# First expert stage of a two-layer transformer: rows and places of a pair of tiles by one transfer each, and three other loads and stores moved to later tiles

## The reference

```
xn = layernorm(x)
x  = x + linear_attention(xn) + experts_top2(xn)              # layer 0
xn = layernorm(x)
x  = x + block_softmax_attention(xn) + experts_capacity(xn)   # layer 1
```

```
logits = xn @ router_w.T ;  top_vals, top_idx = top_k(logits, 2) ;  top_w = softmax(top_vals)
h = square(relu(xn @ w1[e]))          # 256 -> 512, for the chosen expert e
y = h @ w2[e]                         # 512 -> 256
out[token] = sum over its two experts of top_w * y
```

## Time and profile before

| what | value |
|---|---|
| median of three runs | 743.87 us (742.98 to 746.7) |
| the profiled execution: span from first to last instruction | 743.1 us (the profile gives no other time of it) |
| TensorE (PE) busy | 688.5 us, 93% of the span |
| VectorE (DVE) / ScalarE (ACT) / GpSimd (POOL) busy | 545.0 / 446.2 / 443.7 us |
| TensorE lines of the expert stage: L987 / L951 / L962 / L934 | 111.9 / 86.7 us for the two large ones; L962 and L934 are smaller |
| row loads (L572) and id loads (L576) | 71 each, 128 KB and 0.5 KB |

### The profile page before, as it was taken

The page is one execution under the profiler, slowest core; times in us unless marked ns, Lnnn a source line. Parts: engine busy times, 40 slices in busy tenths (PEclk is TensorE's granted clock), DMA queues, the critical chain, the costliest instruction groups (busy, mean ns, idle before and its releaser), DMA issues.

```text
span 743.1 us, 19839 instructions
## 1 busy us (share of the span) xinstructions
PE 688.5 (93%) x6400; PEld 619.2 (83%) x6400; DVE 545.0 (73%) x1311; ACT 446.2 (60%) x940; POOL 443.7 (60%) x524
## 2 busy tenths in 40 slices
PE   5999998899999899999998999799898899999993
PEld 4898877788999899999977999677677678888883
DVE  5999777766887677878658886699986686666632
ACT  6565476666776677745526888466676664444420
POOL 3577789698997897996422223034354635555363
PEclk9999999999999999999999999899999999999998
DMA  9689752365443434533169985145568755666252
GB/s 255 169 261 290 233 164 65 93 175 133 118 124 113 122 101 135 144 87 113 38 202 302 304 282 171 34 106 127 116 112 205 218 197 136 150 147 163 33 58 28
DMA packets 147015, 111.91 MB, mean 151 GB/s; under 512 B 59361, under 2 KB 137188, under 8 KB 146920
## 3 DMA queue, kind: packets, MB, share of 16 engines
q1 hardware_dynamic: 133720, 84.84, 41.4%
q0 software_dynamic: 12624, 25.35, 13.6%
q10 hardware_dynamic: 576, 0.53, 0.3%
HBM read 66.58 MB, written 40.80 MB: 145 GB/s over the span
## 4 chain that ended last, share of the span: by engine, by line
PE 64%; DVE 8%; issue 5%; ACT 3%; DMA 3%; POOL 2%; SPq 1%; ACTq 1%; POOLq 0%; DVEq 0%
PE banks L987 12%; PE bank L1243 11%; PE bank L951 9%; PE banks L1254 5%; PE bank L1043 5%; PE banks L878 4%; PE bank L962 4%; PE banks L1060 3%; PE bank L934 2%; PE bank L1133 2%; PE bank L1122 1%; PE bank L1150 1%; DVE rw L2031 1%; PE banks L865 1%; PE banks L1219 1%
## 5 line engine op out<-in xcount | busy, mean ns | idle before, releaser
L987 PE MATMUL banks<-r_split,rt_split 128*128 x852 | 111.9, 285 | 4.3 <-ACT rw L1447 1.6
L987 PEld LDWEIGHTS banks<-r_split,rt_split 128*128 128x128 f32 x852 | 105.2, 190 | 6.0 <-issue 5.9
L2385 POOL DMA_INDIRECT ults_by_choice_and_token<-rw,y_id x71 | 80.7, 1137 | 39.8 <-ACT rw L1447 29.1
L1243 PE MATMUL bank<-r_split 128*128 128x512 f32 x384 | 89.6, 391 | 1.3 <-issue 1.1
L951 PE MATMUL bank<-wq_high_or_w_low_split,rt_split 128*128 128x256 f32 x560 | 86.7, 286 | 0.6 <-DVE rt_split L1870 0.6
L2333 POOL DMA_INDIRECT rows_by_expert<-rw,slots x64 | 66.2, 1034 | 32.6 <-issue 16.2
L1243 PEld LDWEIGHTS bank<-r_split 128*128 128x128 f32 x384 | 71.4, 188 | 16.3 <-issue 1.9
L2487 POOL DMA_INDIRECT out_x<-r,idx x32 | 50.2, 1568 | 52.9 <-DVE r L2222 45.2
L951 PEld LDWEIGHTS bank<-wq_high_or_w_low_split,rt_split 128*128 128x128 f32 x560 | 76.0, 189 | 1.1 <-DVE rt_split L1870 1.1
L1895 DVE TENSOR_TENSOR rt_split<-rw,rt_split 128x512 fp32r<-128x512 f32 x71 | 65.2, 949 | 11.4 <-ACT rt_split L1440 11.0
L1870 DVE TENSOR_TENSOR rt_split<-r,rt_split 128x512 fp32r<-128x512 f32 x56 | 49.1, 916 | 17.5 <-ACT rt_split L1369 17.5
(11 more groups left out here) (300 smaller groups left out, 1864.7 us busy)
## 6 DMA issues: line engine op xcount, KB each, us to landing
rt<-in_w SPq DMA_DIRECT2D x24, 512.0 KB, 4.8
rw<-rows_by_expert SPq DMA_DIRECT2D x71, 128.0 KB
r<-in_w SPq DMA_DIRECT2D x16, 512.0 KB, 8.8
rt<-ults_by_choice_and_token SPq DMA_DIRECT2D x32, 256.0 KB, 4.1
rw<-in_x SPq DMA_DIRECT2D x16, 256.0 KB
rw<-x_layer SPq DMA_DIRECT2D x16, 256.0 KB
x_plus_bias<-rw SPq DMA_DIRECT2D x16, 256.0 KB, 3.3
rows_layer<-rt SPq DMA_DIRECT2D x16, 256.0 KB, 2.8
```

What stands on the lines that cost most here:

```text
L987: last = pe.matmul(bank[6 + t % 2][:, 0:D], hidden_T(h, t, c), w[:, ds(e2, 1), o + c * D:o + (c + 1) * D], start=n == 0, stop=n == 3 * HC - 1)
L1243: last = pe.matmul(bank[2 * (hb % 2) + k][:, :], w[:, o:o + P], x[:, s.par, c, :], start=n == 0, stop=n == 3 * DC - 1)
L2385: pool.indirect_dma_start(y0_d[:, :], bass.IndirectOffsetOnAxis(y_id[:, t:t + 1].bitcast(I32), 0), c_y[:, t % XB, :], None, bounds_check=l ...
```

## The change

Tiles of a pair are loaded together: SP reads one row number, issues one transfer of 256 x 256 words (256 KB) and one of 256 ids. Pair transfers use buffers 0 and 1 or 2 and 3, and one semaphore for a pair; ids get two semaphores of their own (`id_in`). The transposition waits for the rows alone, the scatter for the ids alone; a pair's load waits besides that the rows and the ids of the pair two before have landed. The stores of x1 come two steps of SP's loop later (`+ 7`), the loads of x three (`k - 2`), the late constants 22 (t = 34 to 42). The last 15 tiles are loaded one by one as before.

```diff
-        l_step = [max(0, k - 5) for k in o_step] + [46 + 3 * i // 2 for i in range(NT - NE)]
+        l_step = [max(0, k - 2) for k in o_step] + [46 + 3 * i // 2 for i in range(NT - NE)]
...
+        def loads(t):
+            if t < T1:
+                return 2 * (t // 2 % 2), 16 * (t // 4 + 1)
+            return t % XB, 16 * (len(range(t % XB, T1, 4)) if t % 2 == 0 else 0) + 16 * ((t - T1) // XB + 1)
+
+        def places(t):
+            if t < T1:
+                return id_in[t // 2 % 2], 16 * (t // 4 + 1)
+            return id_in[t % 2], 16 * (ND // 2) + 16 * ((t - T1) // 2 + 1)
...
-            def load_rows(t):
-                if t >= XB:
-                    sp.wait_ge(cT_ps, group(t - XB) + 1)
-                    sp.wait_ge(xg_in[t % XB], 32 * (t // XB) - 16)
-                r = first_row(t)
-                load_x0(t, r)
-                load_id(t, r, xg_in[t % XB])
+            def load_rows(t, n):
+                slot, landed = loads(t)
+                sp.wait_ge(cT_ps, group(t - XB + n - 1) + 1)
+                if landed > 16:
+                    sp.wait_ge(xg_in[slot], landed - 16)
+                placed, count = places(t)
+                if count > 16:
+                    sp.wait_ge(placed, count - 16)
+                r = first_row(t, n)
+                load_x0(t, n, r)
+                load_id(t, n, r)
...
-            def load_x0(t, r):
-                sp.dma_start(c_xg[:, t % XB, :], xs0_d[ds(r, P), 0:D]).then_inc(xg_in[t % XB], 16)
+            def load_x0(t, n, r):
+                sp.dma_start(c_xg[:, t % XB:t % XB + n, :],
+                             xs0_d[ds(r, n * P), 0:D].rearrange("(j p) n -> p j n", p=P)).then_inc(xg_in[loads(t)[0]], 16)
...
+                    sp.dma_start(y_id[:, t:t + n].unsqueeze(2),
+                                 xs0_d[ds(r, n * P), D:D + 1].rearrange("(j p) n -> p j n", p=P))\
+                      .then_inc(places(t)[0], 16)
...
-            for t in range(XB):
-                load_x0(t, r_first[t])
-            for t in range(XB):
-                load_id(t, r_first[t], zero_out)
+            for t in range(0, XB, 2):
+                load_x0(t, 2, r_first[t // 2])
+            for t in range(0, XB, 2):
+                load_id(t, 2, r_first[t // 2])
             stored = 0
             for t in range(XB, ST0 + 8):
-                if t < ST0:
-                    load_rows(t)
-                while stored < NE and o_step[stored] + 5 <= t:
+                if t < T1:
+                    if t % 2 == 0:
+                        load_rows(t, 2)
+                elif t < ST0:
+                    load_rows(t, 1)
+                while stored < NE and o_step[stored] + 7 <= t:
                     store_x1(stored)
                     stored += 1
-                if t >= XB + 8:
-                    load_late_const(t - XB - 8)
+                if t >= XB + 30:
+                    load_late_const(t - XB - 30)
...
-                for t in tiles:
-                    pe.wait_ge(xg_in[t % XB], 32 * (t // XB) + 16)
+                slot, landed = loads(tiles[0])
+                pe.wait_ge(xg_in[slot], landed)
...
-                pool.wait_ge(xg_in[t % XB], 32 * (t // XB) + 16)
+                placed, count = places(t)
+                pool.wait_ge(placed, count)
```

More of the change, by code:

```diff
@@ L356, in group @@
             return t // 2 if t < T1 else t - ND
+        def loads(t):
[6 more added lines that the diff above has]
+            return id_in[t % 2], 16 * (ND // 2) + 16 * ((t - T1) // 2 + 1)
+        ALL_ROWS = [max(loads(t)[1] for t in range(ST0) if loads(t)[0] == i) for i in range(XB)]
         def x_tile(i):
@@ L364, in two_layers @@
         xg_in = [sem(f"rows_loaded_{i}") for i in range(XB)]
+        id_in = sem2("row_places_loaded")
         w1_r, cT_ps, cT_sb = sem("w1_copied"), sem("rows_T_in_psum"), sem("rows_T_ready")
@@ L558, in load_late_const, with first_row, load_id @@
                         sp.dma_start(bv1_c[o:o + 32, :], bv1_v[h, g]).then_inc(consts_b, 16)
-            def load_rows(t):
-                if t >= XB:
-                    sp.wait_ge(cT_ps, group(t - XB) + 1)
-                    sp.wait_ge(xg_in[t % XB], 32 * (t // XB) - 16)
-                r = first_row(t)
-                load_x0(t, r)
-                load_id(t, r, xg_in[t % XB])
-            def first_row(t):
-                return sp.value_load(tile_r[0:1, t:t + 1], min_val=0, max_val=(REG - 1) * P)
-            def load_x0(t, r):
-                sp.dma_start(c_xg[:, t % XB, :], xs0_d[ds(r, P), 0:D]).then_inc(xg_in[t % XB], 16)
-            def load_id(t, r, loaded):
+            def load_rows(t, n):
[9 more added lines that the diff above has]
+                load_id(t, n, r)
+            def first_row(t, n):
+                return sp.value_load(tile_r[0:1, t:t + 1], min_val=0, max_val=(REG - n) * P)
+            def load_x0(t, n, r):
+                sp.dma_start(c_xg[:, t % XB:t % XB + n, :],
+                             xs0_d[ds(r, n * P), 0:D].rearrange("(j p) n -> p j n", p=P)).then_inc(xg_in[loads(t)[0]], 16)
+            def load_id(t, n, r):
                 with nc.allow_non_contiguous_dma(reason="one word of a row"):
-                    sp.dma_start(y_id[:, t:t + 1], xs0_d[ds(r, P), D:D + 1]).then_inc(loaded, 16)
+                    sp.dma_start(y_id[:, t:t + n].unsqueeze(2),
+                                 xs0_d[ds(r, n * P), D:D + 1].rearrange("(j p) n -> p j n", p=P))\
+                      .then_inc(places(t)[0], 16)
             def load_tables(i):
@@ L610, in _ @@
             sp.wait_ge(table_r, 2)
-            r_first = [first_row(t) for t in range(XB)]
+            r_first = [first_row(t, 2) for t in range(0, XB, 2)]
             for i in range(NX):
                 sp.wait_ge(sc0_out[i], 16 * TOPK * GT * NG // NX)
-            for t in range(XB):
-                load_x0(t, r_first[t])
-            for t in range(XB):
-                load_id(t, r_first[t], zero_out)
+            for t in range(0, XB, 2):
+                load_x0(t, 2, r_first[t // 2])
+            for t in range(0, XB, 2):
+                load_id(t, 2, r_first[t // 2])
             stored = 0
             for t in range(XB, ST0 + 8):
-                if t < ST0:
-                    load_rows(t)
-                while stored < NE and o_step[stored] + 5 <= t:
+                if t < T1:
[4 more added lines that the diff above has]
+                while stored < NE and o_step[stored] + 7 <= t:
                     store_x1(stored)
                     stored += 1
-                if t >= XB + 8:
-                    load_late_const(t - XB - 8)
+                if t >= XB + 30:
+                    load_late_const(t - XB - 30)
                 for i in range(QB, NT):
@@ L1946, in combine @@
                 t = 2 * u + i
-                dve.wait_ge(xg_in[u % 4], 32 * len(range(u % 4, ST0, XB)) + 16 * (u // 4))
+                dve.wait_ge(xg_in[u % 4], ALL_ROWS[u % 4] + 16 * (u // 4 + 1))
                 dve.wait_ge(dy_in[u % 3], 32 * (u // 3 + 1))
```

2 lines of the change are left out of this document (removed).

## The result

The changed kernel takes 736.53 us in the median of four runs (735.69 to 738.14), the kernel before 744.31 in runs beside it; the ratio is 0.9883, 95% interval 0.9854 to 0.9911. Two more groups of runs gave 0.9908 (0.9886 to 0.9931) and 0.9908 (0.9883 to 0.9933). The forecast was 736.4.

The account below looks back on a forecast made before the run. TensorE bounds the expert stage, so only its idle time can be won: -1.73 - 1.61 - 4.70 + 0.2 + 0.4 = -7.44 from a 743.1 us span gives 735.7, median 736.4 us; 8 in 10 range 733.5 to 740.6.

Parts of the forecast that it names:

- The bound and the cause: Expert stage: TensorE is the bound; its waits for rows come from SP's x1 stores, 39.7 us waiting for VectorE's addition.
- The start: TensorE's wait for rows at 137.86 us goes, as tiles 6 and 7 load before the first store: -1.73 us.
- The other five waits: TensorE's later waits for rows ahead of the transposition go, since loads lead by 10 to 12 us: -4.70 us.
- The result copy: TensorE's wait at 156.92 us for ScalarE's copy goes, as tables held by the first store come earlier: -1.61 us.
- g: How much earlier GpSimd's first two result scatters come: about 4.45 us less what VectorE takes from GpSimd.
- The slack of 2.75 us: TensorE lost only 1.61 of ScalarE's 4.36 us wait for the scatter; the copy's wait goes if g exceeds 3.34.
- The first pair: Start of the row loads: both tiles in one 256 KB transfer, between -0.5 and +0.6 us, taken as +0.2.
- the sign named last: A granted clock that stays up from 118 to 122 us would put the time at the low end.
- VectorE beside GpSimd: VectorE instructions slow down where GpSimd's rotation now fills its old gap: between 0 and +1.0 us, taken as +0.4.
- B: Rival: SP now waits for x1 stores to land before x loads, the five waits stay: 741.1 us, chance 0.10.
- D: Rival: late constants in steps 34 to 42 delay row transfers and hold TensorE: slower, 747.5 us, chance 0.04.
- the step from span to median: From the forecast span of 735.7 us to 736.4, keeping the runs' median 0.77 us above the span shown.

Follow-up runs that it names:

- e2: Kernel before with only the x1 stores at +7 and x loads at k-2, single tiles, constants at 12 to 20: 736.84 us, ratio 0.9890.
- e3: Kernel before with the pair transfers alone, stores at +5, x loads at k-5, constants at 12 to 20: 738.73 us, ratio 0.9932.
- e5: The kernel before, run again without edit: 743.77 us, ratio 1.0015.
- e1: The changed kernel, run again without edit: 737.29 us, ratio 0.9908 to the kernel before.
- e8: Changed kernel with four query rotations ahead of the first tile instead of six: 735.17 us, ratio 0.9895 to the kernel before.
- e9: Same edits as e2 on the kernel before, a second time: 736.36 us, ratio 0.9894.
- e4: Changed kernel with the x1 stores back at +5, all else as changed: 739.59 us, ratio 0.9931 to the kernel before.
- e6: Changed kernel with the rows of the first two pairs loaded by one transfer a tile: 735.96 us, ratio 0.9905 to the kernel before.
- e7: Changed kernel with the last query projection ahead of the first transposition: 734.12 us, ratio 0.9891 to the kernel before.
- e10: Changed kernel with the late constants back in steps 12 to 20: 738.99 us, ratio 0.9925 to the kernel before.

## Why the prediction was right, and where its terms were not

- *The bound and the cause.* Right. TensorE's idle time was the limit, SP's ordered wait in the stores the cause: e2 moves the stores and x loads alone, and the rows' waits and 7.7 us go. The order of loads and stores is what matters, and e3 shows a second way to change it.
- *The start, -1.73.* Right: 1.73 and 1.68 us in two traces of before, nothing after.
- *The other five waits, -4.70.* Right in the trace that it was made from, all gone. The second trace of before has 5.7 us there in eight waits, so the kernel loses rather more than 4.70. The lead of 10 to 12 us that was worked out came out as 11 to 15. Of the reasons the shorter blocking is enough; the two steps of lead by pairs are a second cure, not a part of the sum (e3).
- *The result copy, -1.61.* Mis-sized. 0.47, 1.33 and 0.30 us remain in three traces, so about 0.8 went. The step that failed is "both scatters come g earlier, with g about 4.45". The slack of 2.75 us held in some traces (the copy's wait less 2.75 gives 0.59 against 0.47 measured; in e5 1.43 against 1.45) and not in others (e1: 2.16 against 1.33). But g was 1.6. The gap of 4.45 us went; of that, 1.6 us were lost because GpSimd's rotations began later in this trace (117.71 against 116.15 us), and 1.6 because those up to 130.62 ran longer (12.9 us against 11.3 for the same work). The late start was not in the prediction; the longer rotations are its "less what VectorE takes from GpSimd", which it gave no size (that VectorE is the cause is argued, not shown). At g = 1.6 the formula lets the wait stand; that it fell to 0.47 is owed to the scatter's quicker landing, 1.2 us, which no term foresaw. So the two signs named for this part failed: the first scatter near 142 us came at 145.11, and ScalarE's wait under 2.8 us was 3.34, 4.91 and 3.19. The gap itself is no constant of the kernel, it was 0.76 us in e5 with a copy wait of 1.45 all the same. What is left is GpSimd's backlog of eight rotations ahead of its first scatter, which e8 shows by taking two away.
- *The first pair, +0.2.* Nothing: 2.73 to 2.81 us with pairs, 2.66, 2.70 and 3.06 with single tiles (2.73 in e9). The 0.4 us in this term names no row; in the trace of before GpSimd starts 0.43 us behind the landing of its tables (139.33 and 139.76). The clock was rightly not counted as a gain of the change; e5 has no fall there. So the sign named last failed: the clock stayed up from 118 to 122 us and the time was not at the low end.
- *VectorE beside GpSimd, +0.4.* About right: TensorE's waits for VectorE at the start (L951 and L987, 0.59 and 1.60 us before) grew from 2.2 and 2.1 to 2.8 in all three traces, +0.6. That the size fits is in part luck. In the stretch of the old gap VectorE's pair did grow, from 1.28 us to this:

```profile
134.17 2.37 DVE L1895 TENSOR_TENSOR rt_split<-r,rt_split 128x512 fp32r<-128x512 f32 x2
```

But TensorE lost only 0.27 us to it; the rest of the +0.6 lies elsewhere, at 127.64 in this trace and at 146.93 in e1. By the exclusive lock in the Trainium skill, SBUF — State Buffer, "SBUF: two separate sides", the prediction had +1.0; the traces lie between. Not foreseen was the wait of 1.2 us for VectorE near 225 us that e2, e4, e6, e7 and e9 have, and neither before nor the changed kernel.
- *B and D.* SP stood 0.3 us for the landing of x1 stores, and TensorE is busy 50.00 of 50 us where the constants went. The rule that speaks for D (the Trainium skill, DMA: Bandwidth & Descriptors, "Queues, rings and completion order": a semaphore write lands only after the engine's earlier writes) could not show in rows that lead by 11 us or more. The scatter's 6.0 us in e10 would agree with it, the 3.5 us in e2 beside the same constants would not, so no run here settles it.
- *The size.* 736.4 against 736.53 is closer than the reasons earn; that much of it is luck. TensorE's idle time fell by 7.2 us, near the sum of 7.44; the stage was 9.9 us shorter, and the rest of the program longer by 1 to 2 us in the traces after. And the step from span to median rests on a misreading: every traced run that has its time on record has it 1.7 to 1.8 us above its span, so the profiled execution of before took about 744.8 us, 0.9 above the median of its runs, and not 0.77 below it. The step amounts to taking 7.44 us from the median, so the number does not suffer, as long as that execution's waits are the usual ones.

## What to carry to other kernels

In an engine that issues in order, look for waits of things that nobody needs soon standing ahead of loads that somebody needs next: a delay of such stores by two steps, with the x loads behind them by three, gave 1% here, as much as the whole change with its merged transfers. Merging transfers and moving the blocking store cured the same wait, so their gains must be tried apart before they are added. A gap taken from one trace is one draw: the 4.45 us of GpSimd and the 1.85 us at the start were 0.76 and 1.09 in the next trace of the same kernel. And a wait can cost more than its length: behind the 2.27 and 2.04 us of e3 and e4 the granted clock was 0.72 and 0.57 for some microseconds.

## What was not expected of the hardware

Two VectorE instructions took 3.51 us in place of 1.29 while GpSimd ran short elementwise instructions back to back (e4, 223.64 us): the second waited through three of them. In e4 VectorE's pair began 0.8 us ahead of the first of these; in the changed kernel's trace it began 2.2 us ahead (222.69 and 224.90 us) and was done in 1.29. There GpSimd's instructions took 1.2 us each in place of 0.75, and the next pair 1.61. So which of the two engines gave way went with their phase, and where VectorE did, TensorE waited 1.2 us.

The granted clock fell in one of two traces behind the same idle time of TensorE, 1.71 us at the same place of the stage: 0.58 from 130 to 134 us in e10, 1.00 in e2. The 24 matmuls behind it took 4.74 and 3.51 us.
